# A first attention step with another order of its work, and one bf16 product of constant tables in front of each of its first 42 score halves for the row maxima

## The chip, the cores and the metric

The kernel runs on 1 core of one Trainium2 chip. The metric is the device time of one execution in microseconds, a median over repeated executions. A change of this kernel by less than about 0.5% can't be told from none.

## What is computed

Two layers on x of shape (2, 2048, 256). The first is a state-space mixer and a sign-weight product. The second normalises, then adds an ALiBi attention and a second transformer block (RoPE attention with shared key heads, then a router with 8 experts). The change touches only the attention part, which runs both attentions, 16 heads each:

```python
scores = einsum("bhqd,bhkd->bhqk", Q, K) / sqrt(16)      # 2 batches x 16 heads, 2048 x 2048
scores = scores + slopes * (k - q)                        # ALiBi in the first attention, RoPE on Q, K in the second
scores = where(k <= q, scores, -inf)
out    = einsum("bhqk,bhkd->bqhd", softmax(scores), V)
```

## The kernel before

The program has stages one after another: `front` (state space), `middle` (projections, up to 320 us of the profile), `attention` (320 to about 1780 us), `after` and `experts`. `attention` is 16 steps (`STEPS`). A step takes one batch, four heads and one of the two attentions; the heads sit as two pairs, and the two heads of a pair use rows 0 to 63 and 64 to 127 of the TensorE array.

A step does its softmax with the row maximum known beforehand. For this TensorE computes the scores twice. First as "maxima" (order letter m, `max_half`, L1429): one bank of queries by 512 keys, from which VectorE takes the row maximum (`maximum`, L1595 for tiles on the causal diagonal, L1598 for the others). The last maximum of a block of 512 queries releases the turn of the row tops: GpSimd splits them into two parts (`parts`, L1357 and L1359), TensorE transposes them (letter r, `turn_rows`, L1456), ScalarE copies the rows (letter w, L1533), and a DMA from SyncE's queue writes them into two rows of the query operand (L1283). Then come the "scores" (letter s, `score_half`, L1440, with the mask products L1410 on the diagonal): the product over the operand that holds the row tops gives score minus maximum, and ScalarE takes the exponential from the bank (L1545). TensorE multiplies the exponentials by the values (letter v, `values_of`, L1506), 32 array columns to a head, four heads side by side. Letters o, t and d are the copy, the transposition (L1515) and the division of the output.

A letter m is one half: one head of a pair. Halves for the two heads of a pair follow each other and use different rows of the array. An m or an s takes the next of 7 PSUM banks (`RING`), and `take` makes TensorE wait until the bank's last use is read: an m or s seven places further on in the order waits for VectorE or ScalarE to have read this one.

The order in which each engine goes through all this is a string of letters, the same for every engine: `ORDER` for steps 1 to 15 and `FIRST_ORDER` for step 0. Work runs ahead: in every step VectorE is already 42 pairs of maxima (`LEAD`) into the next step's, so step 0 has 220 m where the others have 136, and its beginning has nothing but m. There are four blocks of 512 queries (`NQB`). The first score of a block waits for the DMA of its row tops: `pe.wait_ge(s_mr[qb], ...)`.

GpSimd goes through the same string. In step 0 it also issues the loads of the operands of step 1 in it: at the m with numbers 40, 50, 60 and so on, it first waits until TensorE has issued that many maxima, and issues two DMAs; `parts` of the row tops stand behind these in its queue.

Two tables that lie in SBUF through all this are `fill` and `after_q[0]`, `after_q[1]` (bf16, 128 x 128, zeros and ones), which the mask products use. `middle` ends with 36 products of the identity by itself (`keep_going`, L77).

Of the kernel before, what the change touches and what calls it, by code (L numbers as in the profile page):

```python
# [16 lines left out]
P = 128  # L17
# [984 lines left out]
WIDE = 512  # L1002
RING = 7
NPB = 20
LEAD = 42
# [18 lines left out]
def max_banks():  # L1024
# [42 lines left out]


FIRST_ORDER = (
    "mmmmmmmmmmmmmmmmmrmwmsmmmmmsmmmmmsmmmsmmmmvmmvmmmmmrwsmmmsvsmmommsmmssmmmssmmmssmmvsmmss"  # L1070
    "mmssmsmmmvmmmsmsmmsvsmmmsmvmsmmmmrvmmwmmmvsmssmvsmssmsosmmmsmmsmmmmvsmsmsssmsmmsssmsmmms"
    "tdvmmmsmmsvmsmmvsmsmmvmmmmsmsvssmmmssmmvvmssmsmmmsmvmtmrwmdmmmvsssmmmssmvsmsmsmsosmsmmsm"
    "vssmmmsvmssmsmmmsmsmvsmssmsmmssmrsmmsmwvmsmmmsvmssmssmmmssmmvmsmmvsmmmsmrmwmvsmsmvmsmssm"
    "vtsdmsmvsmsmmsvmmsmsvmsmmsmvmsmmsmmsmmvmosmmmstrdw"
# [3 lines left out]
def diagonal_score(n):  # L1078

    return SCORES[n // 2 % NSP][1]  # L1080
# [35 lines left out]
def attention(nc, A, M):  # L1116
# [4 lines left out]
    with ExitStack() as ctx:  # L1121
# [3 lines left out]
        def sem(name):  # L1125
            return nc.alloc_semaphore(name)

        ps, ident = M["ps"], M["ident"]
# [4 lines left out]
        fill, after_q = M["fill"], M["after_q"]  # L1133
# [32 lines left out]
        s_ex = sem("att_exp_done")  # L1166
# [9 lines left out]
        NSC = 2 * NSP  # L1176
        EX0, OE0, TT0, TE0, RT0, RE0, MP0, TOP0, MD0, HI0 = 16, 1, 2, NQB, 1, NQB, 1, NQB, 512, 2
# [14 lines left out]
        def slot_sem(t):  # L1192

            return t if t < 2 else 2 + (t - 2) % 3

        def filled(t):

            return 1 if t < 2 else (t - 2) // 3 + 1

        def work_of(t):  # L1200
            return FIRST if t == 0 else LAST if t == STEPS - 1 else WORK
# [6 lines left out]
        def max_row(r):  # L1208

            return DOTS if r >= NGB else DOTS + SLOPED  # L1210
# [185 lines left out]
        def _(pe):  # L1396
# [20 lines left out]
            def take(bank, *released):  # L1417

                if bank in holder:
                    pe.wait_ge(*holder[bank])  # L1420
                holder[bank] = released

            def max_half(r, n, bank):

                j = n % 2
                part = slice(HALF * j, HALF * j + max_row(r))
                for p, qt, k0, w, col in MAXES[n // 2 % NMX][2]:
                    kp = 0 if r >= NGB else p
                    ins = pe.matmul(ps[bank][:, col:col + w], q_op[r % 3][part, p, qt * P:(qt + 1) * P],  # L1429
                                    k_op[r % 3][part, kp, k0:k0 + w], start=True, stop=True)  # L1430
                ins.then_inc(s_mt, 1)
# [13 lines left out]
            def values_of(n):  # L1445

                pairs = GROUPS[n][2]
                return [(2 * i + j, j, tiles[x]) for x in range(len(pairs[0])) for i, tiles in enumerate(pairs)
                        for j in range(2)]

            def turn_rows(t, n, bank):

                pe.wait_ge(s_mp, t * NQB + (n + 1 + MP0))
                of_tile = mpart[:, :, :, :].bitcast(F32).rearrange("p j c (h k) -> p (j c h) k", h=PAIRS)
                for k in range(4):
                    ins = pe.transpose(ps[bank][0:2 * GH, k * P:(k + 1) * P], of_tile[:, :, k], ident[:, :])  # L1456
                ins.then_inc(s_rt, 1)

            pe.wait_ge(s_q[0], NFIRST)
            def step(t):  # L1460
                o = t % 3
                for what, n in work_of(t):
                    bank = BANKS[t].get((what, n))
                    if what == "max":
                        if t == 0 and n == 2 * KEYED[0]:
                            pe.wait_ge(s_k[0], NFK)
                        if t == 0 and n == 2 * KEYED[1]:
                            pe.wait_ge(s_k[1], NFK)
                        if n == NMH:

                            pe.wait_ge(s_q[slot_sem(t + 1)], filled(t + 1) * NL)
                        take(bank, s_md, t * NMH + (n + 1 + MD0))
                        max_half(t + n // NMH, n, bank)
                    elif what == "rows":
                        take(bank, s_re, t * NQB + (n + 1 + RE0))
                        turn_rows(t, n, bank)
                    elif what == "score":
                        qb, _, tiles = SCORES[n // 2 % NSP]
                        if n % 2 == 0 and n // 2 % NSP == SFIRST[qb]:

                            pe.wait_ge(s_mr[qb], (t + n // NSC + 1) * NMR)
                        take(bank, s_ex, t * NSC + (n + 1 + EX0))
                        ins = score_half(t + n // NSC, n, bank)
                        if diagonal_score(n):
                            second = BANKS[t][what, n + 1]
                            take(second, s_ex, t * NSC + (n + 2 + EX0))
                            score_half(t + n // NSC, n + 1, second)

                            for ins in mask([ps[b] for b in (bank, second)], tiles, after_q):
                                ins.then_inc(s_sc, 1)  # L1490
                        else:
                            ins.then_inc(s_sc, 1)
                    elif what == "value":
                        qb, _, pairs = GROUPS[n]
                        if n == 0:
                            pe.wait_ge(s_v[slot_sem(t)], filled(t) * 16)
                        if n == VFIRST[qb]:

                            pe.wait_ge(s_oe, t * NQB + (qb + OE0))

                        pe.wait_ge(s_ex, t * NSC + (2 * (PAIR0[n] + len(pairs)) + EX0))
                        at = t * NSC + 2 * PAIR0[n]
                        for slot, j, (p, kt, c0, w, col) in values_of(n):
                            h = 2 * p + j
                            hk = 0 if t >= NGB else h
                            ins = pe.matmul(ps_o[VW * h:VW * h + VW, c0:c0 + w], v_op[o][:, kt, hk * VW:hk * VW + VW],  # L1506
                                            prob[:, (at + slot) % NPB, col:col + w], start=(n == VFIRST[qb]),
                                            stop=(n == VLAST[qb]))
                        ins.then_inc(s_pv, 1)
                    elif what == "turn":  # L1510

                        take(bank, s_te, t * NQB + (n + 1 + TE0))
                        pe.wait_ge(s_oe, t * NQB + (n + 1 + OE0))
                        for j in range(4):
                            ins = pe.transpose(ps[bank][:, j * P:(j + 1) * P],  # L1515
                                               o_sb[n % 2][:, j * P:(j + 1) * P], ident[:, :])
                        ins.then_inc(s_tt, 1)

            for t in range(STEPS):
                step(t)  # L1520
# [1012 lines left out]
```

## Time and profile before

| | |
|---|---|
| median of 3 runs | 2347.92 us (2344.93 to 2354.47) |
| the profiled execution, own time | 2343.51 us |
| its span in the profile | 2341.6 us |
| mean granted clock of TensorE | 0.957 of full |
| PE busy | 2177.9 us (93%) |
| DVE busy | 2029.4 us (87%) |
| ACT busy | 1542.4 us (66%) |
| POOL busy | 670.3 us (29%) |

The page gives busy time of each engine, the span in 40 slices of 58.5 us each, the costliest groups of instructions and the chain of work that ended last. The views of the trace used below are the windows (busy time of each engine in a stretch, and the TensorE clock granted in it, where 1.00 is 2.4 GHz and 0.50 is 1.2 GHz) and the timeline (instructions in order of time, those of one kind merged with their count, with the idle time before them and what ended it). A stretch in which VectorE is busy throughout can't be shortened by another engine, so the idle time of VectorE is what there is to win in attention.

### The profile page before, as it was taken

What the parts mean: (1) busy time and instruction counts of PE and PEld (TensorE: products, weight loads), DVE (VectorE), ACT (ScalarE), POOL (GpSimd) and SP (SyncE); (2) the same over time, 40 slices, a digit from 0 to 9 for tenths busy, and PEclk for the clock granted to TensorE, in tenths of its full rate; (3) what the DMA queues carried; (4) which work ended last, traced back from release to release, by engine and by line L of the source; (5) the groups of instructions that cost most, each with busy time, mean ns of one, the idle gap of its engine ahead of it and who ended that gap; (6) DMA issues with size and microseconds to landing.
All of it is one profiled execution on the core that took longest, in us unless ns stands there. A gap on an engine that the chain in (4) does not pass through costs nothing. (4 is left out here: it accounts for less than half of the span.)

```text
span 2341.6 us, 47819 instructions
## 1 busy us (share of the span) xinstructions
PE 2177.9 (93%) x15840; PEld 1284.0 (55%) x15841; DVE 2029.4 (87%) x5148; ACT 1542.4 (66%) x2993; POOL 670.3 (29%) x996
## 2 busy tenths in 40 slices
PE   4599998999999999999999999999998894999997
PEld 2355554454454444444444444444444783888886
DVE  7799877999999999999999999999991664777775
ACT  3144425688888888888888888888887442444443
POOL 5523003232322322322322222322211254333333
PEclk8799977999999999999999999999999886999999
DMA  5169856564554554442342432432232896444443
GB/s 175 60 218 263 289 169 105 100 131 95 119 86 97 106 99 91 89 82 68 79 90 66 84 85 65 91 85 69 64 90 79 283 305 218 80 79 81 82 81 71
DMA packets 176653, 273.25 MB, mean 117 GB/s; under 512 B 53756, under 2 KB 126204, under 8 KB 170612
## 3 DMA queue, kind: packets, MB, share of 16 engines
q0 software_dynamic: 45936, 137.97, 28.8%
q1 hardware_dynamic: 125476, 122.88, 17.2%
q10 hardware_dynamic: 5044, 9.88, 1.3%
q8 instruction: 110, 1.80, 0.3%
q14 instruction: 87, 0.71, 0.1%
HBM read 128.64 MB, written 140.98 MB: 115 GB/s over the span
## 5 line engine op out<-in xcount | busy, mean ns | idle before, releaser
L1545 ACT ACTIVATE a_p<-banks 128x512 f32<-128x512 f32 x2176 | 1131.1, 608 | 257.7 <-PE banks L1440 205.9
L1598 DVE TENSOR_REDUCE a_mx<-banks 128x1 f32<-128x512 f32 x1536 | 943.3, 679 | 16.9 <-PE banks L1429 16.8
L1506 PE MATMUL banks<-a_p,a_v 128*32 128x512 f32 (+3 forms) x5120 | 588.9, 544 | 1.5 <-ACT a_o L1563 1.1
L1429 PE MATMUL banks<-a_k,a_q 52*128 52x512 f32 (+5 forms) x1600 | 447.0, 414 | 1.9 <-DVE a_rowtop L1595 0.3
L1440 PE MATMUL banks<-a_q,a_k 50*128 50x512 f32 (+7 forms) x1600 | 415.7, 396 | 1.1
L1595 DVE CUSTOM_DVE_ANT_0 a_masked<-banks,later 128x512 bf16<-128x512 f32 (+3 forms) x768 | 330.6, 483 | 12.0 <-PE banks L1429 10.1
L1440 PEld LDWEIGHTS banks<-a_q,a_k 54*128 54x128 f32 (+1 forms) x1600 | 227.1, 185 | 198.5 <-DVE a_mx L1598 95.6
L1429 PEld LDWEIGHTS banks<-a_k,a_q 52*128 52x128 f32 (+1 forms) x1600 | 224.1, 185 | 118.1 <-DVE a_mx L1598 55.6
L1429 PE MATMUL banks<-k,q 52*128 52x512 f32 (+5 forms) x960 | 275.8, 431 | 3.0 <-PEq L482 0.7
L1440 PE MATMUL banks<-q,k 54*128 54x512 f32 (+5 forms) x960 | 255.3, 410 | 10.7 <-DMA q<-a_mrow 9.3
L1440 PEld LDWEIGHTS banks<-q,k 54*128 54x128 f32 (+1 forms) x960 | 137.5, 191 | 137.7 <-DVE a_mx L1598 51.1
L1506 PEld LDWEIGHTS banks<-a_p,a_v 128*32 128x32 f32 x5120 | 109.4, 108 | 174.8 <-issue 126.7
L2184 POOL DMA_INDIRECT out_rows<-e_y,e_token x71 | 111.0, 1564 | 255.4 <-DMA out_rows<-e_y,e_token 198.6
L1429 PEld LDWEIGHTS banks<-k,q 52*128 52x128 f32 (+1 forms) x960 | 140.3, 195 | 76.9 <-DVE a_mx L1598 33.0
L2218 PE MATMUL banks<-w,e_hT 128*128 x568 | 168.0, 397 | 3.1 <-DVE e_hT L2328 3.1
L1410 PE MATMUL banks<-fill,after 64*128 64x128 bf16 (+1 forms) x1280 | 132.4, 214 | 0.0
L1595 DVE CUSTOM_DVE_ANT_0 a_masked<-banks,later,a_mx 128x384 bf16<-128x384 f32 (+3 forms) x256 | 127.2, 543 | 0.4
L2288 ACT ACTIVATE e_w<-w 128x1024 fp32r x71 | 75.3, 1061 | 74.5 <-PE banks L2238 74.4
L2238 PE MATMUL banks<-e_w,e_gT 128*128 128x256 f32 x852 | 118.5, 288 | 1.0 <-DVE e_y L2361 1.0
L2218 PEld LDWEIGHTS banks<-w,e_hT 128*128 128x128 f32 x568 | 102.8, 190 | 23.2 <-issue 4.0
L1357 POOL TENSOR_TENSOR a_mpart<-a_rowtop,a_zeros 128x16 fp32r<-128x16 f32 x64 | 14.7, 229 | 342.6 <-DVE a_rowtop L1602 320.2
L2270 ACT ACTIVATE e_hT<-banks 128x256 fp32r<-128x256 f32 x71 | 27.3, 384 | 124.2 <-PE banks L2205 96.4
(275 smaller groups left out, 2921.3 us busy)
## 6 DMA issues: line engine op xcount, KB each, us to landing
expert_rows<-a_zeros POOLq DMA_DIRECT2D x132, 258.0 KB, 5.2
e_x<-expert_rows SPq DMA_DIRECT2D x71, 129.0 KB, 2.2
expert_rows<-e_y SPq DMA_DIRECT2D x71, 128.0 KB
qa_parts<-m_part SPq DMA_DIRECT2D x16, 512.0 KB, 6.7
ka_parts<-m_part SPq DMA_DIRECT2D x16, 512.0 KB
va_tiles<-m_va SPq DMA_DIRECT2D x8, 1024.0 KB, 6.7
qb_parts<-m_part SPq DMA_DIRECT2D x16, 512.0 KB
a_raww<-in_w POOLq DMA_DIRECT2D x32, 256.0 KB, 5.3
```

The lines of the kernel that those rows point to most:

```text
L1410: ins[j] = pe.matmul(blocks[:, :, HALF * n:HALF * (n + 1)], steps[n][half, :], fill[half, :].unsqueeze(1).to_broadcast([HALF, len(at), HALF]),
L1429: ins = pe.matmul(ps[bank][:, col:col + w], q_op[r % 3][part, p, qt * P:(qt + 1) * P], k_op[r % 3][part, kp, k0:k0 + w], start=True, stop= ...
L1440: ins = pe.matmul(ps[bank][:, col:col + w], k_op[r % 3][part, kp, kt * P:(kt + 1) * P], q_op[r % 3][part, p, qb * QB + c0:qb * QB + c0 + w ...
L1506: ins = pe.matmul(ps_o[VW * h:VW * h + VW, c0:c0 + w], v_op[o][:, kt, hk * VW:hk * VW + VW], prob[:, (at + slot) % NPB, col:col + w], star ...
L1545: nc.scalar.activation(prob[:, (t * NSC + n) % NPB, :], ps[bank][:, :], ACT.Exp, scale=SCALE).then_inc(s_ex, 1)
L1595: ins = v.tensor_tensor_reduce(masked[:, j, col:col + w], ps[bank][:, col:col + w], later[:, WIDE - w:WIDE], 1.0, least, ALU.add, ALU.max, ...
L1598: ins = v.tensor_reduce(top, ps[bank][:, :], AX.X, ALU.max)
L2184: pool.indirect_dma_start(out=out, out_offset=bass.IndirectOffsetOnAxis(ap=token[n % R][:, :], axis=0), in_=y[n % R][:, :], in_offset=None ...
L2218: ins = pe.matmul(bank[:, :], hT[c][s][:, k, :], of[:, ds(at, 1), part * FFN:(part + 1) * FFN].rearrange("p o m -> p (o m)"), start=(k == ...
L2238: ins = pe.matmul(ps_y[:, 0:D], gT[c][s][:, f, :], w2p[of][s][:, f, :], start=(f == 0 and c == 0 and of == 0), stop=(f == FT - 1 and c == 1))
L2270: nc.scalar.activation(hT[0][s][:, :, :].rearrange("p k t -> p (k t)"), ps_h[:, 0:D], ACT.Copy).then_inc(s_hi, 1)
L2288: return nc.scalar.activation(w2p[0][s][:, :, :], w2[:, ds(e * FT, FT), :], ACT.Copy)
```

## The change

It has three parts, all in step 0 and all in `attention`.

1. `FIRST_ORDER` has the same letters in another order. 220 m, 120 s and all others keep their number. Behind the first w stand 5 m instead of 1 before the first s, behind the second w 7 m instead of 3 before the second s, and behind the third w 6 m instead of 3 before the next v and s. In return some later runs of m are shorter.
2. In front of each of the first 42 halves of the maxima (`n < WARM`, with `WARM = LEAD` = 42) TensorE does one product of `after_q[0]` (128 rows by 128 columns) and `after_q[1]` read four times over, 512 bf16 columns. It is written into the bank that the half then overwrites. It is issued behind the wait for the bank.
3. In front of the first score of blocks 0, 1 and 2, TensorE does four such products into the bank of this score. The wait for the bank (`take`) now stands ahead of the wait for the row tops' DMA, and the four products stand between the two.

That is 42 + 12 = 54 products more, and no instruction more on any other engine.

```diff
 FIRST_ORDER = (
-    "mmmmmmmmmmmmmmmmmrmwmsmmmmmsmmmmmsmmmsmmmmvmmvmmmmmrwsmmmsvsmmmommsmmssmmmssmmmssmmvsmmss"
-    "mmssmsmmmvmmmsmsmmsvsmmmsmvmsmmmmrvmmwmmmvsmssmvsmssmsosmmmsmmsmmmmvsmsmsssmsmmsssmsmmms"
+    "mmmmmmmmmmmmmmmmmrmwmmmmmsmmmmsmmmsmmmsmmmvmmvmmmmmrwsmmmmmmmsvsmomsmmssmmssmmssmmvsmmss"
+    "mmssmsmmmvmmmsmsmmsvsmmmsmvmsmmmmrvmmwmmmmmmvsssmvsssmsosmmsmmsmmmmvsmsmsssmsmmsssmsmmms"
...
+            WARM = LEAD
+
+            def light(bank, count):
+
+                for _ in range(count):
+                    pe.matmul(ps[bank][:, :].rearrange("p (b c) -> p b c", c=P), after_q[0][:, :],
+                              after_q[1][:, :].unsqueeze(1).to_broadcast([P, WIDE // P, P]), start=True, stop=True)
+
...
                         take(bank, s_md, t * NMH + (n + 1 + MD0))
+                        if t == 0 and n < WARM:
+                            light(bank, 1)
                         max_half(t + n // NMH, n, bank)
...
                         qb, _, tiles = SCORES[n // 2 % NSP]
+                        take(bank, s_ex, t * NSC + (n + 1 + EX0))
                         if n % 2 == 0 and n // 2 % NSP == SFIRST[qb]:
+                            if t == 0 and qb < 3:
+                                light(bank, 4)
 
                             pe.wait_ge(s_mr[qb], (t + n // NSC + 1) * NMR)
-                        take(bank, s_ex, t * NSC + (n + 1 + EX0))
                         ins = score_half(t + n // NSC, n, bank)
```

TensorE at the beginning of step 0, in the kernel before. All are maxima of the first block; a tile on the diagonal of 384 columns and one of 128 make one half:

```order
118 L1429 MATMUL banks<-k_49,q 128x384
119 L1429 MATMUL banks<-k_49,q 128x128
120 L1429 MATMUL banks<-k_49,q 128x384
121 L1429 MATMUL banks<-k_49,q 128x128
122 L1429 MATMUL banks<-k_49,q 128x512 x2
```

The same place after it, where the maxima are at L1437 and the added products at L1428:

```order
118 L1428 MATMUL banks<-after 128x512
119 L1437 MATMUL banks<-k_49,q 128x384
120 L1437 MATMUL banks<-k_49,q 128x128
121 L1428 MATMUL banks<-after 128x512
122 L1437 MATMUL banks<-k_49,q 128x384
123 L1437 MATMUL banks<-k_49,q 128x128
124 L1428 MATMUL banks<-after 128x512
125 L1437 MATMUL banks<-k_49,q 128x512
```

A product over all 128 rows now stands between any two halves, also between the two of a pair.

TensorE from the second turn of row tops (L1456) to the first score of the second block, before. That score is row 172, and the row above it of L1440 belongs to the first block:

```order
164 L1456 MATMUL banks<-ident,a_mpart 8x128 x4
165 L1440 MATMUL banks<-q,k_49 128x256 x4
166 L1410 MATMUL banks<-fill,after 128x2x64 x4
167 L1429 MATMUL banks<-k_49,q 128x512
168 L1429 MATMUL banks<-k_49,q 128x384
169 L1429 MATMUL banks<-k_49,q 128x128
170 L1429 MATMUL banks<-k_49,q 128x384
171 L1429 MATMUL banks<-k_49,q 128x128
172 L1440 MATMUL banks<-q,k_49 128x512
```

The same stretch after (L1464 is the turn, L1448 a score):

```order
229 L1464 MATMUL banks<-ident,a_mpart 8x128 x4
230 L1448 MATMUL banks<-q,k_49 128x256 x4
231 L1410 MATMUL banks<-fill,after 128x2x64 x4
232 L1437 MATMUL banks<-k_49,q 128x512
233 L1437 MATMUL banks<-k_49,q 128x384
234 L1437 MATMUL banks<-k_49,q 128x128
235 L1437 MATMUL banks<-k_49,q 128x384
236 L1437 MATMUL banks<-k_49,q 128x128
237 L1437 MATMUL banks<-k_49,q 128x512 x4
238 L1428 MATMUL banks<-after 128x512 x4
239 L1448 MATMUL banks<-q,k_49 128x512
```

Four more halves and four of the added products now stand between the turn and the score that waits for the DMA.

## Rows read from the trace of the kernel before

**Rows 1.** The page, busy tenths of VectorE and granted clock in 40 slices.

```profile
DVE  7799877999999999999999999999991664777775
PEclk8799977999999999999999999999999886999999
```

**Rows 2.** Windows: length, busy us (instructions) of PE, PEld, DVE, ACT, POOL; PEclk, DMA, GB/s.

```profile
322.46:334.93 12.47, 8.74 (x27) 4.30 (x23) 12.47 (x47) 1.87 (x2) 0.44 (x2) 0.58 0.97 219
334.93:353.74 18.81, 17.19 (x84) 9.44 (x84) 15.75 (x40) 4.34 (x8) 2.19 (x5) 0.50 0.08 16
353.74:372.00 18.26, 15.31 (x81) 9.35 (x81) 11.16 (x29) 8.78 (x16) 2.60 (x5) 0.50 0.63 91
372.00:400.00 28.00, 24.01 (x165) 11.16 (x163) 25.39 (x61) 14.99 (x29) 10.00 (x18) 0.94 0.69 99
400.00:450.00 50.00, 47.29 (x304) 22.99 (x301) 45.78 (x133) 32.00 (x62) 13.58 (x24) 0.90 0.61 111
450.00:480.00 30.00, 28.38 (x227) 12.69 (x223) 29.48 (x74) 19.67 (x38) 4.80 (x11) 1.00 0.33 68
500.00:580.00 80.00, 79.37 (x674) 39.23 (x672) 79.14 (x218) 66.09 (x129) 21.92 (x39) 1.00 0.49 103
```

**Rows 3.** Timeline of VectorE and TensorE: the waits on DMA and maxima in step 0.

```profile
335.01 0.80 PE L1440 MATMUL banks<-q,k 54*128 54x512 f32 x2 [3.24 <-DMA q<-a_mrow]
350.66 3.08 DVE L1598 TENSOR_REDUCE a_mx<-banks 128x1 f32<-128x512 f32 x5 [1.23 <-PE banks L1429]
355.55 0.69 DVE L1598 TENSOR_REDUCE a_mx<-banks 128x1 f32<-128x512 f32 x1 [1.81 <-PE banks L1429]
358.88 0.79 PE L1440 MATMUL banks<-q,k 54*128 54x512 f32 x1 [2.94 <-DMA q<-a_mrow]
361.48 4.87 DVE L1598 TENSOR_REDUCE a_mx<-banks 128x1 f32<-128x512 f32 x8 [3.87 <-PE banks L1429]
371.48 0.42 DVE L1595 CUSTOM_DVE_ANT_0 a_masked<-banks,later 128x256 bf16<-128x256 f32 x1 [1.42 <-PE banks L1429]
390.55 1.29 DVE L1598 TENSOR_REDUCE a_mx<-banks 128x1 f32<-128x512 f32 x2 [0.78 <-PE banks L1429]
392.37 0.56 DVE L1595 CUSTOM_DVE_ANT_0 a_masked<-banks,later 128x384 bf16<-128x384 f32 x1 [0.52 <-PE banks L1429]
```

**Rows 4.** Timeline of TensorE at the upper clock: halves, then values over 128 rows.

```profile
599.85 0.50 PE L1429 MATMUL banks<-a_k,a_q 52*128 52x512 f32 x1
600.19 0.39 PE L1429 MATMUL banks<-a_k,a_q 52*128 52x512 f32 x1
600.42 0.40 PE L1429 MATMUL banks<-a_k,a_q 52*128 52x512 f32 x2
600.75 0.85 PE L1506 MATMUL banks<-a_p,a_v 128*32 128x384 f32 x8
...
385.17 1.07 PE L1506 MATMUL banks<-a_p,a_v 128*32 128x512 f32 x8
386.16 0.95 PE L1429 MATMUL banks<-k,q 52*128 52x512 f32 x5
```

**Rows 5.** Timeline of TensorE at the lower clock: the same kinds.

```profile
359.61 1.08 PE L1506 MATMUL banks<-a_p,a_v 128*32 128x256 f32 x8
360.62 0.79 PE L1440 MATMUL banks<-q,k 54*128 54x512 f32 x1
361.64 0.62 PE L1440 MATMUL banks<-q,k 54*128 54x512 f32 x1
362.07 0.82 PE L1429 MATMUL banks<-k,q 52*128 52x512 f32 x2
...
345.38 1.93 PE L1506 MATMUL banks<-a_p,a_v 128*32 128x512 f32 x8
347.25 0.79 PE L1429 MATMUL banks<-k,q 52*128 52x512 f32 x2
```

**Rows 6.** Windows: the entry into attention, at the clock before it fell.

```profile
321.00:324.40 3.40, 2.21 (x16) 1.52 (x15) 1.94 (x9) 0.00 (x0) 0.71 (x2) 1.00 0.60 109
```

More of the change, by code:

```diff
@@ L1069 @@
 FIRST_ORDER = (
-    "mmmmmmmmmmmmmmmmmrmwmsmmmmmsmmmmmsmmmsmmmmvmmvmmmmmrwsmmmsvsmmommsmmssmmmssmmmssmmvsmmss"
-    "mmssmsmmmvmmmsmsmmsvsmmmsmvmsmmmmrvmmwmmmvsmssmvsmssmsosmmmsmmsmmmmvsmsmsssmsmmsssmsmmms"
+    "mmmmmmmmmmmmmmmmmrmwmmmmmsmmmmsmmmsmmmsmmmvmmvmmmmmrwsmmmmmmmsvsmomsmmssmmssmmssmmvsmmss"
+    "mmssmsmmmvmmmsmsmmsvsmmmsmvmsmmmmrvmmwmmmmmmvsssmvsssmsosmmsmmsmmmmvsmsmsssmsmmsssmsmmms"
     "tdvmmmsmmsvmsmmvsmsmmvmmmmsmsvssmmmssmmvvmssmsmmmsmvmtmrwmdmmmvsssmmmssmvsmsmsmsosmsmmsm"
```

## The prediction, made before the changed kernel ran

> **What bounds the kernel now.** I read the page's slices first [rows 1]: the clock of TensorE is granted at 9 tenths or more nearly everywhere in attention, but only 7 in two slices at its start, and VectorE is at 7 to 8 tenths there and at 9 after it. So step 0 of attention is the one place in attention with something to win. The windows say how much [rows 2]. In steady state (500 to 580 us) VectorE is busy for 79.14 of 80 us. From 322.46 to 334.93 it is never idle either. After that it is idle for 18.81 - 15.75 = 3.1 us up to 353.74, then 7.1, 2.6, 4.2 and 0.5 us up to 480. In sum **17.5 us is all that step 0 can give**, 0.75% of the time. In the stretches with most of it the clock was 0.50.
>
> The timeline says who ends these waits [rows 3]: always a maximum of TensorE, and behind it two causes. One is the DMA of the row tops: TensorE stands 3.24 us before the first score of block 0 and 2.94 us before that of block 1, with the next maxima queued behind, and VectorE runs dry (3.87 us the second time). The other is the pace of TensorE at the lower clock (1.23, 1.42 us) and its queue behind GpSimd's row tops (1.81 us).
>
> **The order.** VectorE takes 0.61 us for a half of a tile off the diagonal (8 in 4.87 us, [rows 3]). Four more halves between the second turn and the score that waits for the DMA cover 2.4 of the 3.87 us. Three more behind the third cover the 0.78 and 0.52 us at 390.55 and 392.37, 1.3 us. Four more behind the first cover the idle time ahead of 350 us, 3.1 - 1.2 = 1.9 us, if TensorE keeps ahead of VectorE. What the moved halves leave thinner later I put at 1 us of cost, between 0 (VectorE has a backlog of up to seven banks) and 2. Alone, the order would give 2.4 + 1.3 + 1.9 - 1 = 4.6 us.
>
> **The products.** No row shows a bf16 product of 512 columns over 128 rows. A half of 512 columns follows the last of its kind after 0.23 us at the upper clock [rows 4] and 0.43 us at the lower (362.07 after 361.64, [rows 5]). The values use all 128 rows: at the lower clock the 256-column group of eight takes 1.01 us and the 512-column one 1.87, so 256 columns in two batches are 0.86 us, 512 columns in one batch 0.86. A product is thus worth 0.23 to 0.43 us at the upper clock and 0.43 to 0.86 at the lower. I take the small ends, since its form is like a half's and not f32; the large ends stay in the range. Below nothing it can only be by what it does to the clock.
>
> The larger part is what the product does to its neighbours. Today the two halves of a pair run side by side: the row at 600.42 has two halves with one start, and 0.33 us later the next work begins. A product over 128 rows between them forbids that, and makes TensorE change the shape of its work twice per half. These changes have prices in the rows:
> - from 128 rows back to a half: eight value products of 512 columns last 0.99 us to the start of the next half (385.17 to 386.16), of which 0.86 is their own (half of the 1.72 at half the clock), so 0.13; at the lower clock 1.87 - 1.72 = 0.15.
> - the first half after it is not preloaded: 0.34 instead of 0.23 to the next (599.85, 600.19, 600.42), so 0.11; at the lower clock 360.62 to 361.64 is 1.02 for two, one of 0.43 and one of 0.59, so 0.16.
> - from a half to 128 rows: 600.42 to 600.75 is 0.33 instead of 0.23, so 0.10, which I take for both clocks.
>
> One half with its product is 0.23 + 0.13 + 0.11 + 0.23 + 0.10 = **0.80 us at the upper clock** and 0.43 + 0.15 + 0.16 + 0.43 + 0.10 = **1.27 us at the lower**. VectorE needs 28.22 us (12.47 + 15.75, [rows 2]) for the 43 halves done by 353.74, 0.66 us each. So at either clock TensorE, which was ahead, becomes the bound over these 42 halves. The Trainium skill has a rule that speaks against the change in the same way: TensorEngine Tiling (Array Packing), Key Properties, says "Mode switching requires drain". The rows above are its price here, and by the rule without them the sum has no number.
>
> **The clock.** It fell at the entry: full from 321.0 to 324.4 [rows 6], and 0.50 up to 372 [rows 2], although TensorE was recorded busy for 17.19 of 18.81 us. A busy engine by the profile is therefore not enough. With the product in front, an engine with few columns to stream gets more; but much of the added time is change of shape, in which nothing streams. At the lower clock the mix of a half and a product fills 0.86 of 1.27 us, and half of that with only 64 rows' worth of array. I take the lower clock for the forecast from 324.4 on.
>
> **The sum at the lower clock.** Ahead of the 43rd half TensorE has 42 x 1.27 = 53.3 us, two value groups 2 x 1.87 = 3.7, four products 1.7, four doubled scores of 0.59 = 2.4, one turn like half a value group 0.9: 62.0 us. The first 2.6 us at the upper clock do 3.3 halves instead of 2.0, 1.6 us off. It starts at 321.8, 0.7 us ahead of VectorE's first, and VectorE is 1.4 us behind its last (0.8 for the half, 0.6 for the maximum). So the 43rd maximum ends at 321.8 + 62.0 - 1.6 + 1.4 = 383.6 instead of 353.74: **+29.9 us**. The order's 2.4 and 1.3 us come off, its 1.9 us doesn't (TensorE isn't ahead there), and 1 us comes on: +27.2. The four products before the scores of blocks 1 and 2 lie in TensorE's wait for the DMA (2.94 us against 1.7) and cost nothing; without that cover 3.4 us. GpSimd's loads, queued at the same counts of maxima, move with TensorE, and the turn behind them too; the loads of step 1 are needed much later. From step 1 on nothing is changed, since VectorE is full. 2343.5 + 27.2 = 2370.7 us; the profiled execution lies 4.4 us under the median of its three runs, so I put the forecast a little higher, at **2372 us**.
>
> **Rivals.**
> - *The clock holds.* Then the same count is 42 x 0.80 = 33.6, 2.0, 0.9, 1.4 and 0.4: 38.3 us, and the 43rd maximum ends at 321.8 + 38.3 + 1.0 = 361.1, +7.4. Off come 3.7 of the order, the 1.42 us at 371.48 and, if it holds further on, some 2 of the 4.2 us between 400 and 450; on comes 1: about +1, 2345 us. For it: the entry at full clock, and the dense start. Against: 0.80 us is still above 0.66, and the fall at 324.4. The Trainium skill, TensorE: Matmul & The Clock Gate, What's actually happening, says the throttled state is the default and activity releases it; by that rule the added work lifts the clock, and 2345 us is its time. The trace agrees only in part, by the busy stretch at 0.50.
> - *The clock holds for a part of the 42 halves.* Each half at the upper clock saves 0.47 us; with half of them +13 to +18, 2360 us.
> - *Products and changes of shape are free* (the next weights load beneath a product, 0.23 + 0.23 = 0.46 us a half, under VectorE's 0.66), and the clock holds. Then the idle time goes: 3.1 ahead of 353.74, 0.8 of the 1.81 (a faster turn), 2.4, 1.3, 1.42 and 2, less 1 us: -10, 2334 us against the profiled execution, 2337 with the median. This is the side where it is faster; it decides at 0.66 us a half. Against it is each row with a change of shape.
> - *The product costs its large end*, 0.86 us at the lower clock: 42 x 0.43 = 18 us more, 2390 us.
>
> **How the numbers follow.** Lower clock 0.52 (2372), large end 0.07 (2390), held in part 0.14 (2360), held 0.17 (2345), free 0.10 (2335). The range from 2338 to 2390 leaves out most of the free case and half of the large end, some 12 in 100. A measurement of this kernel can't tell less than 0.5% from no change, 11.7 us, so bounds lie at 2336 and 2360. Faster is half of the free case and a little of the held: 0.07. Slower is the lower clock, the large end and half of the held-in-part: 0.66. The same: 0.27.
>
> **What would show it.** In the profile after: starts of the added products 1.2 to 1.3 us apart at a granted clock of 0.50, or 0.8 at 1.00; VectorE idle between maxima from 323 us on, waiting for TensorE; the 43rd maximum done at about 383 us (353 would be the free case, 361 the held one); behind it the wait ahead of block 1's first score hidden, and VectorE's wait there down from 3.87 to about 1.5 us. Halves at 0.5 us or less apart, or a clock at 1.00 from 324 on, would make the forecast wrong.

## The result, and the profile after

The changed kernel takes **2370.8 us** (median of 4 runs, 2360.24 to 2379.97), the kernel before 2348.79 us in the same comparison: a ratio of 1.0089, with a 95% interval of 1.0066 to 1.0111. It is slower, by 0.9%. The forecast was 2372 us.

This median lies where no execution does. Together with ten more executions of the same kernel (e4 below) there are fourteen times: seven between 2359.25 and 2363.3 us, seven between 2379.45 and 2384.84, none between. The mean granted clock goes with the time: 0.958 to 0.963 in the first seven, 0.948 to 0.955 in the others. The kernel has two courses, by which is meant here how the granted clock runs through step 0, and the profiles caught one of each. The first is that of the changed kernel (own time 2360.24 us, span 2358.4, mean clock 0.960), the second that of e4 (2384.84 us, span 2383.0, 0.948). The profiled execution of before has a span of 2341.6 us. So the two spans to account for are +16.8 and +41.4 us.

The page, busy tenths of VectorE and granted clock in 40 slices of 59 us, changed kernel (it answers to [rows 1]):

```profile
DVE  7799877899999999999999999999991664777775
PEclk8799997899999999999999999999999886999999
```

The low slices have not gone. VectorE has 8, 7, 7, 8 in slices 5 to 8, where before had 8, 7, 7, 9, and the clock, 7 and 7 before in slices 6 and 7, is now 9 and 7. The windows, in the stretches of [rows 2] (length, busy us and instructions of PE, PEld, DVE, ACT, POOL, then granted clock, DMA share, GB/s), for the changed kernel:

```profile
322.46:334.93 12.47, 12.26 (x41) 5.44 (x41) 10.82 (x41) 0.00 (x0) 0.96 (x4) 1.00 0.96 217
334.93:353.74 18.81, 18.81 (x89) 8.22 (x88) 15.27 (x42) 6.21 (x10) 0.00 (x0) 1.00 0.01 3
353.74:372.00 18.26, 15.69 (x92) 8.81 (x92) 12.89 (x28) 5.65 (x11) 3.87 (x8) 0.82 0.55 89
372.00:400.00 28.00, 23.24 (x140) 10.97 (x137) 22.15 (x53) 11.18 (x22) 7.87 (x14) 0.80 0.64 92
400.00:450.00 50.00, 47.44 (x276) 23.93 (x274) 41.21 (x115) 28.93 (x56) 11.78 (x21) 0.74 0.59 109
450.00:480.00 30.00, 28.06 (x199) 12.52 (x195) 27.58 (x68) 19.49 (x37) 8.45 (x16) 0.93 0.42 77
500.00:580.00 80.00, 79.52 (x672) 38.67 (x670) 79.23 (x216) 66.46 (x130) 22.48 (x39) 1.00 0.60 124
```

In this course the clock **held** through the 42 halves: 1.00 up to 353.74, where before had 0.58 and 0.50. TensorE is busy for 18.81 of 18.81 us in the second row. Still VectorE is busy for 129.9 us in the first six rows, against 140.0 before. The second course (e4), first three stretches:

```profile
322.46:334.93 12.47, 11.72 (x38) 5.61 (x36) 6.66 (x30) 0.00 (x0) 0.71 (x2) 0.70 0.94 201
334.93:353.74 18.81, 18.81 (x37) 6.32 (x36) 10.24 (x23) 1.87 (x2) 0.44 (x2) 0.50 0.11 32
353.74:372.00 18.26, 18.26 (x58) 8.05 (x57) 8.43 (x23) 4.34 (x8) 0.00 (x0) 0.50 0.00 0
```

Here it fell at 327.6 us and stayed at 0.50 up to 375.4. What a half and its product cost is seen in the timelines of TensorE (start, length, line; L1428 is the added product, L1437 a maximum). Changed kernel, clock 1.00:

```profile
336.15 0.50 PE L1437 MATMUL banks<-k,q 52*128 52x512 f32 x1
336.58 0.39 PE L1428 MATMUL banks<-after 128*128 128x512 bf16 x1
336.90 0.51 PE L1437 MATMUL banks<-k,q 52*128 52x512 f32 x1
```

The second course, clock 0.50:

```profile
335.51 0.79 PE L1437 MATMUL banks<-k,q 52*128 52x512 f32 x1
336.24 0.61 PE L1428 MATMUL banks<-after 128*128 128x512 bf16 x1
336.78 0.79 PE L1437 MATMUL banks<-k,q 52*128 52x512 f32 x1
```

From maximum to maximum it is 0.75 us at 1.00 (336.15 to 336.90) and 1.27 at 0.50 (335.51 to 336.78). VectorE needs 0.66 on average, so TensorE falls behind it by 0.09 or 0.61 us with each half. The timeline of VectorE shows its first maximum, the end of the first 43 halves in the changed kernel, and the largest waits behind them (in brackets the idle time and who ended it):

```profile
323.67 0.56 DVE L1607 CUSTOM_DVE_ANT_0 a_masked<-banks,later 128x384 bf16<-128x384 f32 x1 [3.79 <-PE banks L1437]
...
356.95 3.53 DVE L1610 TENSOR_REDUCE a_mx<-banks 128x1 f32<-128x512 f32 x5 [1.06 <-PE banks L1437]
...
368.13 2.48 DVE L1610 TENSOR_REDUCE a_mx<-banks 128x1 f32<-128x512 f32 x4 [2.18 <-PE banks L1437]
...
400.27 0.56 DVE L1607 CUSTOM_DVE_ANT_0 a_masked<-banks,later 128x384 bf16<-128x384 f32 x1 [2.42 <-PE banks L1437]
403.15 1.89 DVE L1610 TENSOR_REDUCE a_mx<-banks 128x1 f32<-128x512 f32 x3 [2.10 <-PE banks L1437]
```

and in the second course:

```profile
325.48 0.56 DVE L1607 CUSTOM_DVE_ANT_0 a_masked<-banks,later 128x384 bf16<-128x384 f32 x1 [3.78 <-PE banks L1437]
...
378.54 3.53 DVE L1610 TENSOR_REDUCE a_mx<-banks 128x1 f32<-128x512 f32 x5 [1.06 <-PE banks L1437]
...
421.30 0.56 DVE L1607 CUSTOM_DVE_ANT_0 a_masked<-banks,later 128x384 bf16<-128x384 f32 x1 [3.02 <-PE banks L1437]
424.20 2.11 DVE L1610 TENSOR_REDUCE a_mx<-banks 128x1 f32<-128x512 f32 x3 [2.13 <-PE banks L1437]
```

The 43rd maximum ends with the group of five: at 356.95 + 3.53 = **360.48** and at 378.54 + 3.53 = **382.07 us**, where before had 353.74. Where attention ends is seen in the timeline of ScalarE, its last nine exponentials. Before:

```profile
1796.04 4.75 ACT L1545 ACTIVATE a_p<-banks 128x512 f32<-128x512 f32 x9 [0.77 <-PE banks L1440]
```

Changed kernel:

```profile
1810.36 4.75 ACT L1557 ACTIVATE a_p<-banks 128x512 f32<-128x512 f32 x9 [0.77 <-PE banks L1448]
```

Second course:

```profile
1832.13 4.77 ACT L1557 ACTIVATE a_p<-banks 128x512 f32<-128x512 f32 x9 [0.77 <-PE banks L1448]
```

That divides the two differences (us). The first row is VectorE's first maximum, at 322.46, 323.67 and 325.48; the steps after step 0 add nothing, because VectorE is full there (79.23 of 80 us): from 495.86 us to the end of attention each turn of row tops starts 14.3 us later than before, to within 0.1 us.

| | changed kernel | second course |
|---|---|---|
| ahead of attention, with the first product | +1.2 | +3.0 |
| to the end of the 43rd maximum | +5.5 | +25.3 |
| from there to the end of attention | +7.6 | +7.8 |
| the stages behind attention | +2.5 | +5.3 |
| span | +16.8 | +41.4 |

The first and last rows lie outside what the change touches, apart from the first product's 0.3 us.

### The profile page after: what moved, and what is told of

Its sections match the earlier page's. It is cut to its first block and busy times, and to the rows that moved or that the text cites. A ratio compares the mean times of both kernels' runs of the same rounds, so it can differ in the third digit from the quotient of the medians.

```text
span 2358.4 us, 47931 instructions
## 1 busy us (share of the span) xinstructions
PE 2199.5 (93%) x15898; PEld 1290.0 (55%) x15899; DVE 2033.1 (86%) x5148; ACT 1542.3 (65%) x2993; POOL 671.6 (28%) x996
## 5 line engine op out<-in xcount | busy, mean ns | idle before, releaser
L1437 PE MATMUL banks<-a_k,a_q 52*128 52x512 f32 (+5 forms) x1600 | 448.4, 415 | 1.9 <-DVE a_rowtop L1607 0.3
L1448 PE MATMUL banks<-a_q,a_k 50*128 50x512 f32 (+7 forms) x1600 | 416.5, 396 | 0.1
L1448 PEld LDWEIGHTS banks<-a_q,a_k 54*128 54x128 f32 (+1 forms) x1600 | 226.9, 185 | 197.9 <-DVE a_mx L1610 103.1
L1437 PEld LDWEIGHTS banks<-a_k,a_q 52*128 52x128 f32 (+1 forms) x1600 | 225.0, 186 | 119.5 <-DVE a_mx L1610 56.1
L1437 PE MATMUL banks<-k,q 52*128 52x512 f32 (+5 forms) x960 | 277.4, 424 | 1.2 <-DVE a_mx L1610 0.2
L1448 PE MATMUL banks<-q,k 54*128 54x512 f32 (+5 forms) x960 | 256.1, 414 | 7.5 <-DMA q<-a_mrow 6.2
L1448 PEld LDWEIGHTS banks<-q,k 54*128 54x128 f32 (+1 forms) x960 | 138.5, 192 | 134.4 <-DVE a_mx L1610 52.2
L1437 PEld LDWEIGHTS banks<-k,q 52*128 52x128 f32 (+1 forms) x960 | 139.0, 191 | 77.4 <-DVE a_mx L1610 31.5
```

Of the source, the lines that this page charges most:

```text
L1448: ins = pe.matmul(ps[bank][:, col:col + w], k_op[r % 3][part, kp, kt * P:(kt + 1) * P], q_op[r % 3][part, p, qb * QB + c0:qb * QB + c0 + w ...
```

## The experiments

Theory A, that of the forecast: TensorE becomes the bound over 42 halves, by the product's stream, by the changes of shape around it, and by the clock. Theory B: the products are cheap and the moved letters cost the time. Theory C: a product simply adds its own streaming time, whatever its rows. The experiments e1 to e4 ran beside one another, as did e5 to e8, e9 and e10, and e11 and e12; each ratio is to the kernel before on the same chip.

**e1: the order alone.** The kernel before, with the new table.

```diff
 FIRST_ORDER = (
-    "mmmmmmmmmmmmmmmmmrmwmsmmmmmsmmmmmsmmmsmmmmvmmvmmmmmrwsmmmsvsmmommsmmssmmmssmmmssmmvsmmss"
...
+    "mmmmmmmmmmmmmmmmmrmwmmmmmsmmmmsmmmsmmmsmmmvmmvmmmmmrwsmmmmmmmsvsmomsmmssmmssmmssmmvsmmss"
...
```

> The new order alone, no products, waits as before. Theory A (TensorE is made the bound by the products, and the clock decides how much): the order alone is a gain, 2 to 6 us under the kernel before, with the clock low from about 324 us on as there. Theory B (the order is what costs: it takes maxima from the stretch behind 370 us, where the changed kernel loses 8 of its 14 us): 5 to 10 us slower than before, with idle time of VectorE between 375 and 480 us above the 7.3 us of before.

2350.14 us (12 runs, 2346.12 to 2354.74) against 2351.81: 0.9993 (0.9982 to 1.0003), or -1.7 us, between -4.2 and +0.7. Theory B is out, and so is a gain of 4.6 us. In the profile the gain is there at block 1 and is given back at block 2. VectorE in e1, the waits of block 1 and of block 2:

```profile
360.55 2.48 DVE L1598 TENSOR_REDUCE a_mx<-banks 128x1 f32<-128x512 f32 x4 [1.30 <-PE banks L1429]
...
391.47 0.56 DVE L1595 CUSTOM_DVE_ANT_0 a_masked<-banks,later 128x384 bf16<-128x384 f32 x1 [2.51 <-PE banks L1429]
394.12 1.89 DVE L1598 TENSOR_REDUCE a_mx<-banks 128x1 f32<-128x512 f32 x3 [1.87 <-PE banks L1429]
```

The 3.87 us of block 1 are 1.30 now. The 0.78 and 0.52 of block 2 [rows 3] are 2.51 and 1.87: there TensorE stands 3.83 us for the DMA of the row tops, and the maxima queued behind it come late.

**e2: the products alone,** in the old order.

```diff
-    "mmmmmmmmmmmmmmmmmrmwmmmmmsmmmmsmmmsmmmsmmmvmmvmmmmmrwsmmmmmmmsvsmomsmmssmmssmmssmmvsmmss"
...
+    "mmmmmmmmmmmmmmmmmrmwmsmmmmmsmmmmmsmmmsmmmmvmmvmmmmmrwsmmmsvsmmommsmmssmmmssmmmssmmvsmmss"
...
```

> The old order with the 42 and the 3 x 4 products. Theory A: slower than before by 15 to 35 us, as much as or more than the whole change, since the order's cover for the DMA waits is missing. Theory B: about the time of before, at most 8 us slower (the delay that the changed kernel has at 353 us).

2372.96 us (5 runs, 2370.57 to 2378.72): 1.0090 (1.0072 to 1.0108), the same as the whole change. The products are the loss. The one profile of e2 (2378.72 us) shows a third course: the clock was at 1.00 up to 341 us and at 0.50 from 342 to 372, and the 43rd maximum ended at 376.47.

**e3: the order and the three times four products ahead of scores,** without those ahead of the maxima.

```diff
-            WARM = LEAD
+            WARM = 0
```

> The changed kernel without the 42 products, with the 3 x 4 in front of the first scores of blocks 0 to 2. Theory A: within 3 us of the order alone, since TensorE waits there for the DMA of the row tops (3.2, 2.9 and 1.7 us in the kernel before) and four products last 1.7 us at the lower clock; 2342 to 2348 us. If the four products delay the scores instead: 1 to 4 us slower than the order alone.

2350.46 us (12 runs): 0.9995 (0.9984 to 1.0006). Of the products, the 42 are the loss; the twelve others cost nothing that can be measured.

**e4: the changed kernel again,** no edit.

> The changed kernel once more, for its spread: its executions lay at 2360, 2362, 2379 and 2380 us. If the two levels are two courses of the clock in step 0, the five new times fall near 2361 and near 2379 again, those near 2379 with a mean granted clock 0.004 to 0.01 lower; and where the profile is of a slow one, it shows 0.50 from about 325 us on with products 1.2 to 1.3 us apart. If the spread lies outside step 0, the times are spread evenly and the clock doesn't go with them.

2372.42 us (10 runs): 1.0085 (1.0055 to 1.0116). Five lie at 2359.25 to 2363.3, five at 2381.53 to 2384.84. Its profile is the second course shown above. The means of the two groups over all fourteen times are 2361.1 and 2382.6 us. The 21.5 us between them are, as far as two profiles tell, the 19.8 us that the 43rd maximum comes later (25.3 - 5.5).

**e5: a product ahead of the first half of each pair only,** 21 in all, so that the two halves of a pair stand side by side again.

```diff
-                        if t == 0 and n < WARM:
+                        if t == 0 and n < WARM and n % 2 == 0:
                             light(bank, 1)
```

> The changed kernel with a product only in front of the first half of each pair (21 instead of 42), so that the two halves of a pair run side by side again and there is one change of shape and back per pair. Theory A (what costs is that a product keeps TensorE on one half at a time and makes it change shape, 0.75 us a half at 1.00 and 1.27 at 0.50): a pair takes about 0.32 + 0.43 = 0.75 us at the upper clock and 1.27 at the lower, against 1.3 us of VectorE, so TensorE is no longer the bound: 0 to 10 us over the order alone, of which the lower clock makes the most, and no second level of times. Theory C (each product simply adds its time, whatever stands beside it): half of the loss of the changed kernel, 10 to 12 us over before.

2352.19 us (12 runs) against 2346.64: 1.0016 (1.0004 to 1.0028). Half the products leave about a quarter of the loss of 22 us. TensorE in e5, clock 1.00:

```profile
326.18 0.49 PE L1437 MATMUL banks<-k,q 52*128 52x512 f32 x2
326.60 0.39 PE L1428 MATMUL banks<-after 128*128 128x512 bf16 x1
326.92 0.49 PE L1437 MATMUL banks<-k,q 52*128 52x512 f32 x1
```

The two halves of a pair start together, and from pair to pair it is 326.92 - 326.18 = 0.74 us, 0.37 for a half: at 1.00 TensorE is no longer the bound. At 0.50 a pair takes 1.27 us (334.15 to 335.42), 0.63 for a half, just under VectorE's 0.66.

**e6: 42 products over 64 rows,** the rows that the following half uses. No change of shape is left.

```diff
-            def light(bank, count):
+            def light(bank, count, part=slice(0, P)):
...
-                    pe.matmul(ps[bank][:, :].rearrange("p (b c) -> p b c", c=P), after_q[0][:, :],
-                              after_q[1][:, :].unsqueeze(1).to_broadcast([P, WIDE // P, P]), start=True, stop=True)
+                    pe.matmul(ps[bank][:, :].rearrange("p (b c) -> p b c", c=P), after_q[0][part, :],
+                              after_q[1][part, :].unsqueeze(1).to_broadcast([rows, WIDE // P, P]), start=True, stop=True)
...
-                            light(bank, 1)
+                            light(bank, 1, slice(HALF * (n % 2), HALF * (n % 2) + HALF))
```

> The changed kernel with the 42 products over 64 rows, those of the half that follows, so the array isn't used in another shape. Theory A: 0.43 us a half even at the lower clock, under VectorE's 0.66: VectorE is not kept waiting in the first 42 halves; within 4 us of the order alone, and no second level of times. Theory C: the same loss as the changed kernel, 2360 us and more, since as many columns are streamed.

2347.41 us (11 runs): 1.0001 (0.9991 to 1.0011). The same 512 columns, at half the rows, cost nothing. Theory C is out. It isn't the clock alone that saves e6: it fell to 0.50 there too, from 331 to 341 us, and still VectorE was busy for 6.00 of the 6.00 us from 331 to 337, where the changed kernel needs 1.27 us a half.

**e8: two such products per half,** as many rows times columns as the change streams.

```diff
-                            light(bank, 1, slice(HALF * (n % 2), HALF * (n % 2) + HALF))
+                            light(bank, 2, slice(HALF * (n % 2), HALF * (n % 2) + HALF))
```

> As the last, with two products over 64 rows in front of each of the 42 halves: as many rows times columns as one over 128 rows, without the change of shape. Theory A: about 0.6 us a half at the upper clock and up to 1.3 at the lower if the three follow one another, 0.43 and 0.86 if the next half starts beside the last of the three: 0 to 4 us over the order alone where the clock holds, 8 to 25 where it falls. If the change of shape is no cost of its own, the starts of the maxima are as far apart as in the changed kernel, 0.75 us at 1.00.

2345.80 us (12 runs): 0.9997 (0.9985 to 1.0009). No loss either. TensorE in e8 (L1429 the products, L1438 the maxima):

```profile
326.10 0.57 PE L1438 MATMUL banks<-k,q 52*128 52x512 f32 x1
326.28 0.60 PE L1429 MATMUL banks<-after 64*128 64x512 bf16 x2
326.53 0.58 PE L1438 MATMUL banks<-k,q 52*128 52x512 f32 x1
```

Two products and a half take 0.43 us (326.10 to 326.53), less than one product over 128 rows and a half (0.75). Most other steps are longer, 0.6 to 0.8 us, since VectorE sets the pace there (from 324.14 to 349 us it waits for no maximum); the closest of them is 0.50 (332.42 to 332.92). So with as many rows times columns, some 0.25 to 0.32 us a half is the change of shape together with the lost overlap of work on the two halves of the rows. These runs don't divide it further.

**e7: 42 products over 128 rows, a quarter of the columns.** The changes of shape stay, the stream goes.

```diff
-            def light(bank, count):
+            def light(bank, count, w=WIDE):
...
-                    pe.matmul(ps[bank][:, :].rearrange("p (b c) -> p b c", c=P), after_q[0][:, :],
-                              after_q[1][:, :].unsqueeze(1).to_broadcast([P, WIDE // P, P]), start=True, stop=True)
+                    pe.matmul(ps[bank][:, 0:w].rearrange("p (b c) -> p b c", c=P), after_q[0][:, :],
+                              after_q[1][:, :].unsqueeze(1).to_broadcast([P, w // P, P]), start=True, stop=True)
...
-                            light(bank, 1)
+                            light(bank, 1, P)
```

> The changed kernel with 128 instead of 512 columns in each of the 42 products (the 3 x 4 stay). Theory A: the products' own stream falls by 0.16 us a half at the upper clock and 0.32 at the lower, the change of shape stays: maxima start 0.59 us apart at 1.00 and 0.95 at 0.50. With the clock at 0.50, since little is streamed: 42 x (0.95 - 0.66) = 12 us over the order alone, 2358 to 2366 us; with it at 1.00, about the order alone. Theory C: the loss is a quarter of the changed kernel's, 5 us over before.

2364.41 us (6 runs, 2359.07 to 2367.24): 1.0072 (1.0055 to 1.0090). Most of the loss stays. TensorE in e7, clock 0.50:

```profile
329.70 0.79 PE L1437 MATMUL banks<-k,q 52*128 52x512 f32 x1
330.42 0.29 PE L1428 MATMUL banks<-after 128*128 128x128 bf16 x1
330.64 0.79 PE L1437 MATMUL banks<-k,q 52*128 52x512 f32 x1
```

0.94 us from maximum to maximum. With a quarter of the columns 0.33 of 1.27 us go; 0.94 are still above VectorE's 0.66. All six times lie together here, and the clock was at 0.50 from 324.9 to 376.1 in the one profile.

**e9: two products over 64 rows per half up to the 42nd, then one up to half 130,** with `light` as in e6 and all else as in the changed kernel.

```diff
-                        if t == 0 and n < WARM:
-                            light(bank, 1)
+                        if t == 0 and n < 130:
+                            light(bank, 2 if n < WARM else 1, slice(HALF * (n % 2), HALF * (n % 2) + HALF))
```

> Two products over 64 rows in front of each of the first 42 halves as in the one before, and one in front of each of the halves 42 to 129, where that kernel's clock fell between 380 and 411 us. If the loss behind 388 us is the clock's: 0.50 vanishes there, VectorE's delay doesn't rise again, 2340 to 2344 us, 0.1 to 0.3% under the kernel before. If TensorE's stream is what is short there, the 88 more products of 0.21 us cost as they stand: 2348 to 2358.

**2338.19 us** (6 runs, 2334.92 to 2340.65) against 2345.76: 0.9969 (0.9956 to 0.9981), faster than both kernels. The gain of 0.31% is under the 0.5% at which single comparisons of this kernel begin to tell something; it rests on the interval and on the profile below, which agree. The windows of e9:

```profile
322.46:334.93 12.47, 12.47 (x74) 6.53 (x71) 12.47 (x48) 1.87 (x2) 0.44 (x2) 1.00 0.95 209
334.93:353.74 18.81, 17.46 (x149) 9.23 (x147) 17.66 (x50) 5.99 (x11) 2.15 (x6) 1.00 0.22 30
353.74:372.00 18.26, 16.86 (x140) 9.40 (x139) 17.10 (x43) 12.12 (x23) 4.47 (x8) 1.00 0.71 112
372.00:400.00 28.00, 26.47 (x215) 13.33 (x214) 25.42 (x58) 16.45 (x33) 11.10 (x20) 1.00 0.78 122
400.00:450.00 50.00, 45.48 (x323) 21.41 (x322) 45.69 (x133) 30.86 (x59) 11.94 (x21) 0.97 0.63 110
450.00:480.00 30.00, 28.27 (x230) 13.87 (x226) 28.88 (x71) 20.40 (x39) 10.13 (x18) 1.00 0.32 81
```

The clock is 1.00 but for one dip of 3.4 us, and VectorE is busy for 147.2 us of the 157.5, where before had 140.0: 7.2 us less idle. VectorE in e9, its waits at blocks 1, 2 and 3:

```profile
356.53 2.48 DVE L1611 TENSOR_REDUCE a_mx<-banks 128x1 f32<-128x512 f32 x4 [0.64 <-PE banks L1438]
...
385.00 1.89 DVE L1611 TENSOR_REDUCE a_mx<-banks 128x1 f32<-128x512 f32 x3 [0.60 <-PE banks L1438]
387.27 1.29 DVE L1611 TENSOR_REDUCE a_mx<-banks 128x1 f32<-128x512 f32 x2 [0.38 <-PE banks L1438]
...
423.31 0.56 DVE L1608 CUSTOM_DVE_ANT_0 a_masked<-banks,later 128x384 bf16<-128x384 f32 x1 [3.36 <-PE banks L1438]
```

The last of these was 1.28 us before (at 431.33). TensorE stands 3.42 us there for the DMA of block 3's row tops, up to 421.94, and the one dip of the clock follows. e11 below, with the old order, has 3.00 us there, so it isn't the new order that opens this wait.

The last nine exponentials of attention in e9:

```profile
1788.57 4.77 ACT L1558 ACTIVATE a_p<-banks 128x512 f32<-128x512 f32 x9 [0.78 <-PE banks L1449]
```

7.5 us earlier than before, and the median is 7.6 us lower.

**e10: e8 with the old order; e11: e9 with the old order.** The edit is the table alone, as in e2.

> Two products over 64 rows in front of each of the first 42 halves, with the old order. Theory A (the order's new runs of maxima cover the DMA waits where TensorE is ahead of VectorE): 2 to 6 us slower than the same with the new order, since the waits of 1.6 and 3.9 us come back, and still at or under the kernel before by the clock. If the new order is worth nothing beyond block 1, as the run with the order alone had it (+0.7 us at the end of the step in its profile): the same time as with the new order within 2 us.

2345.28 us (11 runs): 0.9998 (0.9989 to 1.0007). Without the longer row of products the order is worth nothing here either (e8 0.9997).

> Products over 64 rows as in the longer variant (two for each of the first 42 halves, one for each of halves 42 to 129), with the old order. With the clock at 1.00 nearly throughout, what is left between the orders is the order itself: Theory A: 2 to 6 us slower than with the new order (the maxima that cover the waits on the DMA of the row tops in blocks 0, 1 and 2). If the clock alone made the gain: the same within 2 us.

2343.38 us (11 runs) against 2345.82: 0.9990 (0.9980 to 1.0000). The new order (e9, 0.9969) is about 5 us better; the two intervals just meet, the two ran in different comparisons, and in the profile of e11 the clock was at 0.50 for 17 us against 3.4 in e9, so a part of the 5 us is the clock's. e12 below is the closer comparison. VectorE in e11 at block 1:

```profile
360.08 4.90 DVE L1611 TENSOR_REDUCE a_mx<-banks 128x1 f32<-128x512 f32 x8 [3.77 <-PE banks L1438]
```

That is the wait of 3.87 us of [rows 3], still there although the clock was at 1.00 up to this point but for one dip of 3.4 us; in e9 it is 0.64.

**e12: e9 without the three times four products.**

```diff
-                            if t == 0 and qb < 3:
-                                light(bank, 4)
```

> The longer variant with the new order and without the 3 x 4 products over 128 rows in front of the first scores. If they are hidden in the waits on the DMA and don't move the clock: the same within 2 us. If they keep the clock up at the turns of row tops: 0.50 appears behind one of them (about 336, 358 or 392 us) and the time rises by 2 to 6 us. If they cost: 1 to 3 us faster.

2340.13 us (11 runs): 0.9976 (0.9967 to 0.9986). The intervals of e9 and e12 overlap, so the 2 us between them are not shown. Its profile has three dips of the clock, of 3.4 us at 358.4, 6.8 at 423 and 6.8 at 443.7, 17 us in sum as in e11. e11 and e12 ran side by side and differ in the order and the twelve products alone: 2343.38 and 2340.13 us, so with the same time at 0.50 the new order is worth 3.3 us, if the twelve products cost nothing as in e3.

## Why the prediction was right, and where it was not

The sign and the size of the total were right, the size partly by luck: 2372 us was the time of one course by the working, and it is the middle of two courses.

**The price of a half with its product: right.** The working had 0.80 us at the upper clock and 1.27 at the lower, all from rows without such a product; 0.75 and 1.27 were measured. Of its parts, from a half to the next product it had 0.44 us (0.23 + 0.11 + 0.10) and 0.43 was found (336.15 to 336.58); from the product to the half 0.36, and 0.32 was found (336.58 to 336.90). The prices of change of shape taken from values and halves carried over to a bf16 product here. That the 128 rows between the halves are the costly part, and not the columns, is shown by e6 and e8 (no loss) against e7 (most of it). The rule of the Trainium skill (TensorEngine Tiling (Array Packing), Key Properties) that a change of mode requires a drain agrees; e8 against the changed kernel, 0.43 and 0.75 us, is what a half pays for it and for the halves that can't overlap.

**The 43rd maximum: right in both courses.** Forecast 383.6 at the lower clock and 361.1 with the clock held; measured 382.07 and 360.48, with entries that were 2.7 and 0.9 us later than before's 321.80. Taken from the entry, both came 4.2 and 1.5 us earlier than the working had it. In the held course 42 times 0.05 us, 2.1, covers it; in the other the clock was back at 1.00 from 375.4, for the last seven halves or so, 0.5 us each.

**The clock: half right.** The forecast gave the lower clock 0.52 and the held clock 0.17. They came seven times each. The step that failed is the treatment of one execution's clock as a property of the kernel: that it falls "from 324.4 on". With the products it fell there in half of the executions, and in e2's profile 14 us later. What decides it isn't shown. The Trainium skill's rule (TensorE: Matmul & The Clock Gate, What's actually happening), that activity releases the clock, agrees with the held course and with e8 and e9, and not with the second course, where TensorE was recorded busy all through 334.93 to 353.74 at 0.50.

**The stretch behind the 43rd half: wrong, by 10 to 14 us.** The sum had -2.7 us at the lower clock (order -2.4 and -1.3, thinner later maxima +1), and about -6 with the clock held. Measured: +7.8 and +7.6. This is the larger part of why the held course came in at 2360 and not at 2345 us, and the lower one at 2384. The turns of row tops divide it. The table has the time from turn to turn, less that of before, and in brackets how long the clock was at 0.50 in it (us). The 2nd to 4th turns are those of blocks 1 to 3 in step 0, before at 353.00, 384.64 and 425.48; the 7th is at 481.57 before, and behind it the difference stays.

| | 2nd to 3rd turn | 3rd to 4th | 4th to 7th |
|---|---|---|---|
| before | 0 (19.2) | 0 (10.2) | 0 (3.4) |
| changed kernel | -0.8 (17.1) | +4.3 (17.1) | +3.8 (13.6) |
| second course | -2.0 (17.1) | +5.2 (20.5) | +4.0 (13.6) |
| e1, order alone | -2.1 (17.1) | +4.2 (13.6) | -0.8 (0) |
| e3, order and twelve products | -2.1 (17.1) | +4.2 (13.6) | +3.8 (13.6) |
| e9 | -4.9 (0) | -2.0 (0) | +2.6 (3.4) |

The mis-sized terms are two:

- *The order, at block 2.* Its first part came: the wait of block 1 is 2.18 us instead of 3.87 (about 1.5 was forecast), in e1 1.30. The 1.3 us of block 2 did not come off; they became 2.42 and 2.10 us (rows at 400.27 and 403.15), and 3.02 and 2.13 in the second course. "1 us, between 0 and 2" for thinner later maxima was too little: TensorE reaches block 2's score sooner and stands longer for its DMA, 2.99 us in the changed kernel and 3.83 in e1, where before had 1.68. The third to fourth turn takes 2.7 to 5.6 us longer in all eight profiles with the new order and without e9's longer filler, with 13.6 to 20.5 us at 0.50; it takes 0 to 0.5 us longer in the three with the old order (before, e2, e10), with 9 to 10 us. It is a cost of the order, and e1 has it without any product.
- *The clock from the fourth turn on,* which the sum at the lower clock left as it was. There the changed kernel, e1 and e3 do the same work, and with 13.6 us at 0.50 it takes 4.5 us more than with none:

```profile
425.48:481.57 56.09, 51.94 (x381) 24.49 (x381) 53.66 (x151) 38.31 (x73) 14.01 (x27) 0.97 0.39 73
436.01:495.86 59.85, 55.73 (x385) 25.94 (x385) 54.25 (x151) 38.64 (x73) 14.05 (x27) 0.89 0.37 69
426.94:482.27 55.33, 50.99 (x381) 23.54 (x380) 53.56 (x151) 38.23 (x73) 14.03 (x27) 1.00 0.40 74
427.56:487.44 59.88, 55.73 (x385) 25.94 (x385) 54.25 (x151) 38.61 (x73) 13.98 (x27) 0.89 0.37 69
```

These are the windows of before, the changed kernel, e1 and e3. So these 3.8 us don't need the 42 products: e3 has them in its profiled execution (2355.47 us, the slowest but one of its twelve), e1 in its own (2348.64) hasn't. Nor do they need the new order: e2 has 3.6, also with 13.6 us at 0.50. With one profile for each, how often they come isn't known, and why the clock falls there isn't settled.

At block 2 the order's cost needs the clock too. e9 has the same order, with a small product ahead of each maximum up to half 130; the clock is at 1.00 from the third to the fourth turn, the stretch is 2.0 us shorter than before, and the waits at block 2 are 0.60 and 0.38 us. Whether the clock falls because TensorE stands there, or TensorE stands longer by the clock, these runs don't separate. In the held course the clock had fallen at 365.4, when TensorE had just stood 1.73 us for block 1's DMA.

**The order alone: wrong.** The forecast was -4.6 us, e1 has -1.7 (0.9993, between -4.2 and +0.7). With the clock mostly at 1.00 it is worth 3.3 us (e12 against e11) to 5 (e9 against e11), so the rows were read rightly, and a condition was missing.

**The twelve products ahead of scores: right,** nothing (e3). TensorE in the changed kernel at block 1:

```profile
362.76 1.04 PE L1428 MATMUL banks<-after 128*128 128x512 bf16 x4
365.53 0.79 PE L1448 MATMUL banks<-q,k 54*128 54x512 f32 x1 [1.73 <-DMA q<-a_mrow]
```

The four lie in the wait, of which 1.73 us still stand behind them.

**The rivals.** Free products are out (e7, and 0.75 us a half). The large end of the product is out: 1.27 us as with the small end. "Held in part" was not the way to 2360 us; "held" was, with the loss behind it. Held in part is what e2's profile shows, at 2378.72 us.

## What to carry to other kernels

Before you put filler work into a tensor engine to keep its clock, give it the shape of its neighbours: the same columns over 64 rows cost nothing here where those over 128 rows cost 22 us. Compute the engine's time per unit at both clock levels and compare it with that of the engine it feeds; if it is over at the upper level, as here with 0.75 against 0.66 us, a held clock doesn't bring the loss back. And a reordering that moves work ahead of one wait takes its cover from the next, so follow each moved piece to the wait it used to hide.

## What the runs showed of the hardware that was not expected

One kernel on one core had two courses of the clock, seven and seven of fourteen executions, 2361.1 and 2382.6 us on average. In both profiles the clock was 1.00 at the entry; it fell at 327.6 in one and held up to 365.4 in the other. A single profile shows only one of them.

Two bf16 products over 64 rows per half held the clock at 1.00 in 334.93 to 353.74 with TensorE recorded busy for 17.46 of 18.81 us (e9); 17.19 busy us of halves alone ran at 0.50 before, and 18.81 of 18.81 did in the second course of the changed kernel. Busy time in the profile doesn't tell which it will be.
